# A graph-attention kernel on one core: the slot table from one side first, behind three products, with smaller first loads and the first V reductions behind the counts

## What is computed

```python
x1 = relu(x @ W_ah + b_ah)
def gat_conv(x, src, dst, W, a_src, a_dst, b):
    h = (x @ W).reshape(N, H, C)
    as_n = (h * a_src).sum(-1)
    ad_n = (h * a_dst).sum(-1)
    e = leaky_relu(as_n[src] + ad_n[dst], 0.2)
    m = segment_max(e, dst, num_segments=N)
    p = exp(e - m[dst])
    s = segment_sum(p, dst, num_segments=N)
    alpha = p / (s[dst] + 1e-16)
    return segment_sum(alpha[:, :, None] * h[src], dst, num_segments=N) + b
xs = [relu(gat_conv(x1, src, dst, W, a_s, a_d, b)) for W, a_s, a_d, b in layers]
out = layernorm(x + relu(concatenate(xs, axis=1) @ W_out + b_out))
```

## Time and profile before

| | |
|---|---|
| time, median of 3 runs (lowest to highest) | 956.46 us (956.26 to 956.62) |
| the profiled execution's own time | 956.7 us |
| its span | 955.1 us |
| busy in the span: PE | 933.2 us (98%) |
| PE's weight loads | 865.8 us (91%) |
| DVE | 739.1 us (77%) |
| ACT | 367.5 us (38%) |
| POOL | 45.9 us (5%) |

### The profile page before, as it was taken

The page is one execution under the profiler, slowest core; times in us unless marked ns, Lnnn a source line. Parts: engine busy times, 40 slices in busy tenths (PEclk is TensorE's granted clock), DMA queues, the critical chain, the costliest instruction groups (busy, mean ns, idle before and its releaser), DMA issues.

```text
span 955.1 us, 14393 instructions
## 1 busy us (share of the span) xinstructions
PE 933.2 (98%) x5584; PEld 865.8 (91%) x5584; DVE 739.1 (77%) x1064; ACT 367.5 (38%) x534; POOL 45.9 (5%) x94
## 2 busy tenths in 40 slices
PE   6999999999999999999999999999999999999997
PEld 2677649999999999999999999999999779999996
DVE  6999986999999299998999999988877282243233
ACT  1666323122212255375465555555555540011000
POOL 4700000000000000000010010010010100000000
PEclk9999999999999999999999999999999999999999
DMA  5350722534453723144253352239341353223111
GB/s 174 50 197 22 259 85 89 168 108 152 130 163 92 227 75 95 56 108 106 82 123 63 94 131 67 71 101 374 93 121 42 101 161 127 81 91 116 68 33 33
DMA packets 57693, 108.16 MB, mean 113 GB/s; under 512 B 14013, under 2 KB 41246, under 8 KB 56487
## 3 DMA queue, kind: packets, MB, share of 16 engines
q1 hardware_dynamic: 39188, 66.22, 22.7%
q0 software_dynamic: 5360, 18.77, 7.7%
q10 hardware_dynamic: 13090, 22.44, 7.5%
HBM read 80.34 MB, written 27.08 MB: 112 GB/s over the span
## 4 chain that ended last, share of the span: by engine, by line
PE 56%; ACT 0%; DVE 0%; issue 0%; ACTq 0%
PE ps L1302 34%; PE ps L1382 18%; PE ps L1372 2%; PE ps L1337 2%; ACT R_XIN L733 0%; PE ps L1287 0%; DVE R_XIN L1118 0%; DVE stats L1108 0%; DVE R_EXP L1104 0%; DVE R_EXP L1102 0%; ACT rstd L785 0%; DVE mv L1113 0%; DVE rstd L1115 0%; ACTq L732 0%; ACTq L762 0%
## 5 line engine op out<-in xcount | busy, mean ns | idle before, releaser
L1302 PE MATMUL ps<-R_W 125*125 125x193 f32 x2400 | 395.2, 327 | 1.2 <-issue 0.8
L1302 PEld LDWEIGHTS ps<-R_W 125*125 125x125 f32 x2400 | 391.7, 188 | 1.8 <-issue 1.1
L707 ACT ACTIVATE R_W<-R_EXP,s 125x1250 f32<-125x1250 f32 x120 | 160.3, 1340 | 155.0 <-PE ps L1302 74.7
L998 DVE SCALAR_TENSOR_TENSOR R_W<-R_W,R_CNT 125x1250 f32<-125x1250 f32 x120 | 174.5, 1455 | 3.0 <-DVE R_EXP L987 1.7
L957 DVE CUSTOM_DVE_ANT_0 R_ROWS<-R_MASK,R_ROWS 125x1250 bf16<-125x1250 bf16 x100 | 138.6, 1456 | 3.2 <-ACTq L660 3.2
L1230 PE MATMUL ps<-Wl_hi,x_hi 128*125 128x384 f32 x360 | 122.1, 339 | 0.0
L1230 PE MATMUL ps<-Wl_hi,x_lo 128*125 128x384 f32 x360 | 121.7, 338 | 0.0
L1230 PE MATMUL ps<-Wl_lo,x_hi 128*125 128x384 f32 x360 | 121.6, 338 | 0.0
L1382 PE MATMUL ps<-Wo_hi,xs_hi 128*125 128x384 f32 (+2 forms) x324 | 109.5, 338 | 0.3 <-PE ps L1372 0.3
L1382 PE MATMUL ps<-Wo_lo,xs_hi 128*125 128x384 f32 (+2 forms) x324 | 109.4, 338 | 0.0
L1382 PE MATMUL ps<-Wo_hi,xs_lo 128*125 128x384 f32 (+2 forms) x324 | 109.2, 337 | 0.0
(11 more groups left out here) (146 smaller groups left out, 824.8 us busy)
## 6 DMA issues: line engine op xcount, KB each, us to landing
xs_dram<-R_XIN POOLq DMA_DIRECT2D x18, 625.0 KB, 8.6
h_dram<-R_HOUT ACTq DMA_DIRECT2D x30, 336.0 KB
R_W<-h_dram SPq DMA_DIRECT2D x12, 840.0 KB
R_ROWS<-as_dram SPq DMA_DIRECT2D x12, 625.0 KB, 4.4
R_EXP<-u_dram SPq DMA_DIRECT2D x6, 1250.0 KB, 7.8
R_X<-u_dram SPq DMA_DIRECT2D x6, 1250.0 KB, 5.6
R_ROWS<-in_W_all SPq DMA_DIRECT2D x18, 384.0 KB, 3.4
Wo_sb<-in_W_out POOLq DMA_DIRECT2D x1, 6912.0 KB, 27.0
```

Of the source, the lines that this page charges most:

```text
L707: nc.scalar.activation(prob[r % PSLOTS], expo[:, r % XSLOTS], ACT.Exp, bias=s02[:, r % NT, ds(2 * p + r // NT, 1)]).then_inc(S["exp_done"], 1)
L998: nc.vector.scalar_tensor_tensor(out=prob[r % PSLOTS], in0=prob[r % PSLOTS], scalar=HUGE, in1=cntT[:, r % NT, 0:N], op0=ALU.min, op1=ALU.m ...
L1302: ins = mm(ps[0:PT, o:o + HW], prob[(q * NT + j) % PSLOTS][:, t * PT:(t + 1) * PT], hB[:, q, j], start=(j == 0 and t % 2 == 0), stop=(j == ...
```

## The change

Constants: `V_HEAD` from 1 to 0; `X0_CUTS` cuts the first group's x into four pieces (feature blocks 0, 1, 2 to 3, 4 to 5) instead of three of two blocks; `BEFORE_TABLE` = 3 products stand ahead of the turn of side 0, `BEFORE_LENGTHS` = 7 ahead of the turn of side 1, and the row for the longest window stands behind unit `LENGTHS_AT` = 3.

- ACT's queue: the first 128 columns of W_ah block 0, x block 0, the rest of W_ah block 0, x block 1, x blocks 2 to 3, x blocks 4 to 5, W_ah block 1.
- DVE: only side 0 is compared and folded ahead of its turn; `lowest` and the comparison of side 1 fill the waits; the multiplication and folds of side 1 follow the table; its reduction and the sum follow the first batch's one-hots; the chain for the longest window moves from behind the first batch to behind the second. The eight first V reductions go to the others, behind the last one-hots.
- SP: the two bias loads wait for x block 0; `load_a(0)` is issued behind the slots of the third batch, the first V blocks behind all slots.

```diff
@@ -40,8 +40,13 @@
 X1_HEAD = 12
-V_HEAD = 1
-G0_PARTS = 3
+V_HEAD = 0
+V_LOADS_AT = 2
+X0_CUTS = (0, 1, 2, 4, 6)
+X0_PARTS = list(zip(X0_CUTS, X0_CUTS[1:]))
+BEFORE_TABLE = 3
+BEFORE_LENGTHS = 7
+LENGTHS_AT = 3
 BANK = 512
@@ -296,8 +301,9 @@
         S = {n: sem(n) for n in names}
-        x0_in = [sem(f"x0_in{i}") for i in range(G0_PARTS)]
+        x0_in = [sem(f"x0_in{i}") for i in range(len(X0_PARTS))]
         x_in = [sem(f"x_in{g}") for g in range(len(GROUPS))]
+        wah_first = sem("wah_first")
         wah_in = [sem(f"wah_in{m}") for m in range(KT)]
@@ -346,8 +352,6 @@
             sp.dma_start(e_int, dst.rearrange("o (p e) -> p (o e)", p=PT)).then_inc(S["edges_in"], 16)
-            sp.dma_start(b_ah_sb[:], b_ah).then_inc(S["small_in"], 16)
-            sp.dma_start(b_all_sb[:], b_all).then_inc(S["small_in"], 16)
@@ -363,14 +367,15 @@
-            sp.wait_ge(x0_in[G0_PARTS - 2], 16)
-            load_a(0)
-            for k in range(V_HEAD):
-                load_v(0, k)
+            sp.wait_ge(x0_in[0], 16)
+            sp.dma_start(b_ah_sb[:], b_ah).then_inc(S["small_in"], 16)
+            sp.dma_start(b_all_sb[:], b_all).then_inc(S["small_in"], 16)
...
                 load_slots(sp, mybir.EngineType.SP, w0, mid, win_in[i])
+                if i == V_LOADS_AT:
+                    load_a(0)
@@ -563,12 +568,14 @@
-            load_w_ah(0)
-            for i in range(G0_PARTS):
-                kk = slice(KT // G0_PARTS * i, KT // G0_PARTS * (i + 1))
+            act.dma_start(W_ah_sb[0][:, 0], W_ah[0][:, 0:KP]).then_inc(wah_first, 16)
+            for i, (k0, k1) in enumerate(X0_PARTS):
                 wide = GROUPS[0][1] * PT
-                act.dma_start(xT[0][:, kk].rearrange("p k n -> p (k n)"),
-                              xT_rows[:, kk.start * wide:kk.stop * wide]).then_inc(x0_in[i], 16)
+                act.dma_start(xT[0][:, k0:k1].rearrange("p k n -> p (k n)"),
+                              xT_rows[:, k0 * wide:k1 * wide]).then_inc(x0_in[i], 16)
+                if i == 0:
+                    act.dma_start(W_ah_sb[0][:, 1:KT].rearrange("p k f -> p (k f)"), W_ah[0][:, KP:KT * KP]
+                                  ).then_inc(wah_in[0], 16)
             load_w_ah(1)
@@ -804,25 +811,27 @@
             link(nc.vector.tensor_reduce(highest, groups, axis=AX.X, op=ALU.max))
+            def fold(side):
+                link(nc.vector.tensor_tensor(reach4[:, side], reaches[:, side, :, 0:4], reaches[:, side, :, 4:8], ALU.max))
+                link(nc.vector.tensor_tensor(reach2[:, side], reach4[:, side, :, 0:2], reach4[:, side, :, 2:4], ALU.max))
+                link(nc.vector.tensor_tensor(reach_g[:, side], reach2[:, side], reaches[:, side, :, 8:GP], ALU.max))
+                nc.vector.tensor_tensor(reach[:, side], reach_g[:, side, :, 0], reach_g[:, side, :, 1], ALU.max
+                                        ).then_inc(S["reach_sb"], 1)
+            link(nc.vector.tensor_tensor(reaches[:, 0], over_w(highest), win_lo_g, ALU.is_ge))
+            link(nc.vector.tensor_tensor(reaches[:, 0], reaches[:, 0], over_w(to_end), ALU.mult))
+            fold(0)
             link(nc.vector.tensor_reduce(lowest, groups, axis=AX.X, op=ALU.min))
-            nc.vector.tensor_tensor(reaches[:, 0], over_w(highest), win_lo_g, ALU.is_ge)
+            dve.wait_ge(S["reachT_ps"], 1)
+            nc.vector.tensor_reduce(ab[:, 0:1], bank(2)[0:NW, 0:PT], axis=AX.X, op=ALU.max).then_inc(S["ab_sb"], 1)
             link(nc.vector.tensor_tensor(reaches[:, 1], win_hi_g, over_w(lowest), ALU.is_ge))
-            nc.vector.tensor_tensor(reaches[:, 0], reaches[:, 0], over_w(to_end), ALU.mult)
-            link(nc.vector.tensor_tensor(reaches[:, 1], reaches[:, 1], over_w(group_end), ALU.mult))
-            rows = lambda v: v.rearrange("p s w g -> p (s w) g")
-            link(nc.vector.tensor_tensor(rows(reach4), rows(reaches)[:, :, 0:4], rows(reaches)[:, :, 4:8], ALU.max))
-            link(nc.vector.tensor_tensor(rows(reach2), rows(reach4)[:, :, 0:2], rows(reach4)[:, :, 2:4], ALU.max))
-            link(nc.vector.tensor_tensor(rows(reach_g), rows(reach2), rows(reaches)[:, :, 8:GP], ALU.max))
-            nc.vector.tensor_tensor(reach.rearrange("p s w -> p (s w)"), rows(reach_g)[:, :, 0], rows(reach_g)[:, :, 1],
-                                    ALU.max).then_inc(S["reach_sb"], 1)
-            dve.wait_ge(S["reachT_ps"], 1)
-            link(nc.vector.tensor_reduce(ab[:, 0:2], bank(2)[0:NW, 0:256].rearrange("p (w c) -> p w c", w=2)[:, :, 0:PT],
-                                         axis=AX.X, op=ALU.max))
-            nc.vector.tensor_tensor(ab[:, 2:3], ab[:, 0:1], ab[:, 1:2], ALU.add).then_inc(S["ab_sb"], 1)
             dve.wait_ge(S["rows_ps"], 1)
...
                                     ).then_inc(S["table_sb"], 1)
+            link(nc.vector.tensor_tensor(reaches[:, 1], reaches[:, 1], over_w(group_end), ALU.mult))
+            fold(1)
@@ -883,6 +892,12 @@
                 if i == 0:
+                    dve.wait_ge(S["reachT_ps"], 2)
+                    dve.wait_ge(S["ab_sb"], 1)
+                    link(nc.vector.tensor_reduce(ab[:, 1:2], bank(2)[0:NW, 128:128 + PT], axis=AX.X, op=ALU.max))
+                    nc.vector.tensor_tensor(ab[:, 2:3], ab[:, 0:1], ab[:, 1:2], ALU.add).then_inc(S["ab_sb"], 1)
+                if i == 1:
+                    dve.wait_ge(S["rows_ps"], 2)
                     link(nc.vector.tensor_reduce(longest[0:1, 0:1], bank(3)[0:1, NW:2 * NW], axis=AX.X, op=ALU.max))
@@ -1166,30 +1181,44 @@
                         pe.wait_ge(S["turn_sb"], i - 2)
-                    pe.wait_ge(wah_in[m], 16)
+                    pe.wait_ge(wah_first if i == 0 else wah_in[m], 16)
                     if g > 0:
                         pe.wait_ge(x_in[g], 16)
-                if i == 0 and k % (KT // G0_PARTS) == 0:
-                    pe.wait_ge(x0_in[k // (KT // G0_PARTS)], 16)
+                if i == 0 and k == 1:
+                    pe.wait_ge(wah_in[0], 16)
+                if i == 0 and k in X0_CUTS:
+                    pe.wait_ge(x0_in[X0_CUTS.index(k)], 16)
                 ins = mm(bank(5 + i % 3)[:, 0:w], W_ah_sb[m][:, k], xT[g][:, k],
...
-            for s in range(KT // G0_PARTS):
+            def reach_turn(side):
+                pe.wait_ge(S["reach_sb"], side + 1)
+                nc.tensor.transpose(bank(2)[0:NW, side * 128:side * 128 + PT], reach[:, side], ident[0:PT, 0:PT]
+                                    ).then_inc(S["reachT_ps"], 1)
+            def table_row(column):
+                pe.wait_ge(S["ab_sb"], 1 if column == 0 else 2)
+                o = 0 if column == 0 else NW
+                mm(bank(3)[0:1, o:o + NW], ab[:, column:column + 1], ident[0:NW, 0:NW], start=True, stop=True
+                   ).then_inc(S["rows_ps"], 1)
+            for s in range(BEFORE_TABLE):
                 x1_step(s)
-            pe.wait_ge(S["reach_sb"], 1)
-            for w in range(2):
-                ins = nc.tensor.transpose(bank(2)[0:NW, w * 128:w * 128 + PT], reach[:, w], ident[0:PT, 0:PT])
-            ins.then_inc(S["reachT_ps"], 1)
-            pe.wait_ge(S["ab_sb"], 1)
-            mm(bank(3)[0:1, 0:NW], ab[:, 0:1], ident[0:NW, 0:NW], start=True, stop=True)
-            mm(bank(3)[0:1, NW:2 * NW], ab[:, 2:3], ident[0:NW, 0:NW], start=True, stop=True).then_inc(S["rows_ps"], 1)
-            for s in range(KT // G0_PARTS, X1_HEAD):
+            reach_turn(0)
+            table_row(0)
+            for s in range(BEFORE_TABLE, BEFORE_LENGTHS):
+                x1_step(s)
+            reach_turn(1)
+            for s in range(BEFORE_LENGTHS, X1_HEAD):
                 x1_step(s)
...
                 unit(un)
+                if un == LENGTHS_AT:
+                    table_row(2)
                 for s in range(x1_upto(un - 1), x1_upto(un)):
```

## The result

| | before | after |
|---|---|---|
| median | 956.20 us (955.28 to 956.62, 22 runs) | 958.64 us (957.12 to 961.54, 22 runs) |
| ratio after / before (95% interval) | | 1.0029 (1.0024 to 1.0035) |
| profiled execution, its span | 956.7, 955.1 | 961.54, 959.9 |

The change costs 2.4 us in the median. The profiled execution of after is the longest of its 22: in it the span grew by 4.8 us. (The one of before, 956.7, also lies at the upper end of its kernel's.) The others show where the spread lies: the three shortest (957.12 to 957.58) ran at a mean granted clock of 0.999, the five longest (959.82 to 961.54) at 0.993 or 0.994. A mean clock alone does not say what a fall cost: of the executions of before in the first group of experiments, one at 0.996 was the shortest (955.12).

The account below looks back on a forecast made before the run. The prediction took DVE's line from the table to the last V reduction as the bound, with PE following. -1.86 + 0.50 + 2.23 = +0.87 us gave a median of 957.3, range 955.2 to 959.2.

Parts of the forecast that it names:

- the sum's own upper end: Whole kernel: the forecast with every term at its high end, a late piece of x included, +2.3 us, 958.7.
- What bounds the start: Start up to the scores: DVE's line from the table to its last V reduction sets when PE's scores begin.
- The rival that V's line isn't what holds them: Before the scores: the 1.10 us wait is PE's own, so moving V reductions is free; -1.36 us, 955.1, chance 0.05.
- Step 1, the table: Start of DVE's line: one side first, table queued behind PE's third product, written at 12.98, 1.86 us earlier.
- Step 2, the second `ab` column: Count loop on DVE: one reduction and the addition now stand behind the first one-hots, +0.50 us.
- Step 3, eight V reductions: Behind the one-hots on DVE: eight V reductions moved there at 0.279 us each, +2.23 us.
- Step 4: Loads: changed issues and order on SP's and ACT's queues cost nothing; V loads have 4.5 us in hand.
- the one stall: V reductions at block 1 of layer 2: the 1.50 us wait behind the layer-weight load stays.
- The slower rival, the clock before the scores: PE's pause before the scores reaches 3.3 us and its clock falls, losing 1.7 to 3.4 us; 959.0 to 960.7, chance 0.10.
- The sum: Whole kernel: -1.86 for the table, +0.50 for the second column, +2.23 for V reductions, together +0.87 us.
- Late small pieces: Loads of x: product 2's piece lands at 10.3, +2.1 us, 958.6, chance 0.10; wholly serial pieces, +7.3, chance 0.02.

Follow-up runs that it names:

- v_head_0_alone: The kernel before with V_HEAD = 0 and nothing else changed: 960.15 us, ratio 1.0048.
- v1e_w2l_t2: The changed kernel with V_HEAD=1, V loads after x block 1, W_ah block 2 after PE's turn, two products not three ahead of the turn: 953.89 us.
- pe_busy: The changed kernel with four unused products between PE's x products and its wait for V: 957.84 us, ratio 1.0021.
- w2_early: The changed kernel with W_ah block 2 loaded right behind block 1 on ACT's queue: 958.45 us, ratio 1.0026.
- w2_busy: The changed kernel with W_ah block 2 loaded right behind block 1 and four unused products before PE's wait for V: 956.79 us, ratio 1.0009.
- pieces_alone: The kernel before with only the smaller first pieces of x and W_ah and PE's waits for them: 955.60 us, ratio 0.9994.
- v1e_w2l_actw: The changed kernel with V_HEAD=1, V loads after x block 1, W_ah block 2 after PE's turn, first layer weights on ACT's queue: 954.83 us.
- v_head_1: The changed kernel with V_HEAD = 1, the first eight V reductions back between table and first key cast: 956.22 us, ratio 1.0003.

## Why the prediction was right, and where it was not

The forecast of 957.3 was 1.3 us low. The time of 958.64 lies within the range of 955.2 to 959.2, but above the bound of 958.37 at which it counts as slower than before, to which the prediction gave 0.21 against 0.73 for "within". The time also lies just under the sum's own upper end of 958.7, but that end stood for a late piece of x, and it was reached in another way. The direction and the line that sets the scores were understood; that the number is this close is in part luck, for an earlier table than forecast made up for a part of what the later slots cost. Step by step:

- **What bounds the start** stood: DVE's line of V sets the scores. PE starts 0.10 us behind V's last read in after as in before. The rival that V's line isn't what holds them is out: with one constant changed in `v_head_0_alone`, V ended and PE began 1.8 us later, both.
- **Step 1, the table.** The mechanism held: the turn stood behind the third product and DVE waited 1.61 us for it, and the runs with two products cut that wait to 0.3 and 0.4 us. The size was off in our favour (12.30, not 12.98). Product 1 started at 7.7, as forecast (7.6), but the granted clock rose at 10.4 instead of 17.0, ahead of the turn: the turn began at 10.72 instead of 11.1 and took 0.27 us, against 0.41 in `v1e_w2l_t2`, where the clock was still low. The clock's rise moves from run to run: with the same start of PE's work it came at 8.6 to 8.9 in `pe_busy`, `w2_early` and `w2_busy`, and the table at 11.5 to 11.6. What failed is the sentence that table end to first cast "is the slots' load and is unchanged": it grew from 4.27 to 5.83 us by the collision with W_ah block 2. A PE that is through its first group earlier also lets ACT issue its next load earlier, and this effect of the change I had not followed. The step gave -0.98, where the sum had -1.86: a miss of 0.88.
- **Step 2, the second `ab` column**: +0.50 forecast; the reduction and the addition are 0.28 and 0.16, and the whole stretch grew by 0.42.
- **Step 3, eight V reductions**: +2.23 forecast and found in the count of reductions. Beside it the stretch grew by 0.56 in the profiled execution, 0.48 of it stalls (0.34 at 104.83 is new, the other 1.64 instead of 1.50). Step 4 had put the waits for V's loads at nothing beyond the one stall; `pe_busy` has a new one too, of 0.74 us.
- **The slower rival, the clock before the scores**, had 0.10 and came true. In the profiled execution the pause was 3.89 us and the scores took 2.65 more, inside the 1.7 to 3.4 that the rival named. The step that failed is "against it: 3.3 is a little shorter". Pauses of 3.13 and 3.23 us were enough in `v_head_0_alone` and `w2_early`, so the last pause of the run was a poor yardstick for where it decides: it shows one moment at which the clock fell, not the shortest pause that makes it fall. In these traces the fall came 2.4 us (after), 2.8 us (`w2_early`) and 4.1 us (`v_head_0_alone`) behind PE's last product. The Trainium skill (TensorE: Matmul & The Clock Gate, Part 1) says that the moment of a transition varies because it depends on a window that runs freely and does not reset when the kernel starts. These three falls, the rises at 8.6 to 10.4 and the mean clocks of after's executions between 0.999 and 0.993 agree with it; if it is so, the same pause may cost in one execution and not in the next.
- **The sum.** In the profiled execution the direct part is +2.23, against +0.87 forecast; the misses are 0.88 (the slots) and 0.56 (the stalls in the main), less 0.08 of step 2. In the profiled execution of `pe_busy` it is +1.67: the cast 1.74 earlier, close to the 1.86 of the sum, for there the table was written 1.46 earlier than forecast, which nearly paid for the collision; what is left of the miss is the V stretch, 0.76 longer than forecast. In the three shortest executions, at a mean clock of 0.999, the whole loss is 0.9 to 1.4 us, so the direct part itself varies. How the others' time divides between stalls and the clock can't be read without their traces; that is open.
- **Late small pieces** did not come true in after: the piece that product 2 needs landed at 8.6, and `pieces_alone` lost nothing. In `v1e_w2l_actw` it landed a microsecond later and PE waited 0.49 us for it. The 2.0 us for each DMA that the prediction took from the Trainium skill (DMA: Bandwidth & Descriptors, on the anatomy of one DMA) are given there for DMAs that GpSimd issues; the loads of x are ACT's, so that sentence did not bear on them.

## What to carry to other kernels

When a change makes an engine early, follow what that engine's next step releases, and put the loads that this brings forward beside the small ones that are on the path: here one prefetch of 384 KB took back 1.5 of the 2.5 us that the table had gained. Work that hides under another wait is worth keeping there, and moving it behind a stage that ends in a pause of TensorE is paid twice, once for the work and once for the clock. A bound read from a single long pause says nothing of the shortest one that costs.

## What was not expected of the hardware

- The clock fell while PE was at work with short waits. In `v_head_1` it fell at 23 us, behind waits of 1.82 and 0.42 us, with PE busy for 1.74 of the 3 us ahead:

```profile
20.00:23.00 3.00, 1.74 (x18) 1.00 0.64 146
23.00:29.80 6.80, 6.19 (x24) 0.50 0.24 15
30.00:34.00 4.00, 3.50 (x32) 1.00 0.24 17
```

  From the first cast to the last one-hots that run took 1.2 us more than after. Most of it is one wait of DVE for PE's row for the longest window, which after doesn't have:

```profile
28.98 0.26 DVE L903 TENSOR_REDUCE longest<-ps 1x1 int32<-1x105 f32 x1 [1.02 <-PE ps L1208]
```

  So a start made earlier, with PE then waiting for one-hots, has this risk as well.
- In `v_head_0_alone` the clock was still at 1.00 when PE began the scores at 130.87 and fell about 1 us later, while PE was at work. Here the pause was paid after it had ended.
- Small loads suffered from a large one on another queue: a slot of 4 KB took 3.4 instead of 1.8 us beside 384 KB, and V's blocks were stalled 2.4 us by weights on a queue of their own.
